# A two-layer vision tower: GpSimd's long instructions between the halves go to other engines, the routed tables come later, and the end of the routed experts is reordered

## What is computed

```python
h = patches(x) @ tokW + tokb                        # 16x16 patches, 768 -> 256
h = h + sparse_attention(layernorm(h))              # 16 heads; a router keeps 25 of 64 keys per head
h = h + moe(layernorm(h))                           # below
h = h + polymax_attention(layernorm(h))             # causal; 16 heads; score -> (1 + relu(s)**2 or 1 - 0.01 s) / 1000
h = h + ternary_ffn(layernorm(h))                   # RMS norm, w in {-1, 0, 1}, 256 -> 1024, gelu, RMS norm, -> 256

def moe(x):                                         # 8 experts in 4 groups, top 2 groups, top 2 experts
    shared = (silu(x @ sw1.T) * (x @ sw3.T)) @ sw2.T
    routed_in = x[flat_idx] * weights               # rows by the token's own index ...
    h = silu(grouped_mm(routed_in, w1, counts)) * grouped_mm(routed_in, w3, counts)
    return shared.at[flat_idx].add(grouped_mm(h, w2, counts))   # flat_idx holds expert numbers 0..7
```

## Time and profile before

| what | value |
|---|---|
| median of 3 runs | 785.64 us (785.05 to 787.7) |
| profiled execution | 786.8 us, its span 784.6 us |
| PE busy | 684.2 us (87%) |
| DVE busy | 616.3 us (79%) |
| ACT busy | 429.7 us (55%) |
| POOL busy | 114.6 us (15%) |
| mean granted clock of PE | 0.948 of full speed |

### The profile page before, as it was taken

One profiled execution on the slowest core, in us unless ns is written; L12 is line 12 of the kernel. 1 busy time (PEld: TensorE's weight loads), 2 busy tenths in 40 slices (PEclk: granted clock), 3 DMA queues, 4 the chain that ended last, 5 costly groups with the idle time before them and its releaser, 6 DMA issues.

```text
span 784.6 us, 26966 instructions
## 1 busy us (share of the span) xinstructions
PE 684.2 (87%) x11581; PEld 489.3 (62%) x11581; DVE 616.3 (79%) x1349; ACT 429.7 (55%) x661; POOL 114.6 (15%) x95
## 2 busy tenths in 40 slices
PE   5769989999999989987999698899989998798666
PEld 4455676857666675856587375575757676464534
DVE  6768888888898888889796788888889786757643
ACT  4444555464644546366473666849486662936323
POOL 0202111020212111024300421010100101010010
PEclk9889999999999999999978899999999999999959
DMA  9116202002020200020000000000000000000000
GB/s 304 55 31 239 83 0 80 0 0 80 0 80 0 80 0 0 20 91 2 1 3 2 1 7 26 3 29 1 27 0 27 0 4 28 3 29 2 29 1 28
DMA packets 8546, 27.40 MB, mean 35 GB/s; under 512 B 3616, under 2 KB 4384, under 8 KB 6944
## 3 DMA queue, kind: packets, MB, share of 16 engines
q1 hardware_dynamic: 8480, 26.42, 9.4%
HBM read 22.22 MB, written 4.19 MB: 34 GB/s over the span
## 4 chain that ended last, share of the span: by engine, by line
issue 43%; PE 30%; ACT 12%; DVE 10%; POOL 4%; DMA 1%; POOLq 0%; ACTq 0%; DVEq 0%; SPq 0%
PE PS L380 5%; PE PS L727 3%; PE PS L773 3%; ACT w_s L1076 3%; PE PS L761 3%; PE PS L717 2%; PE PS L370 2%; POOL H L1192 2%; PE PS L740 2%; ACT work L1067 2%; ACT xn L1014 1%; PE PS L391 1%; POOL rstd L1175 1%; PE PS L601 1%; PE PS L347 1%
## 5 line engine op out<-in xcount | busy, mean ns | idle before, releaser
L927 ACT ACTIVATE PT<-PS 128x512 f32<-128x512 f32 x64 | 36.6, 596 | 66.0 <-PE PS L479 66.0
L740 PE MATMUL PS<-xT,wqkv_h 128*128 128x512 f16 x256 | 65.1, 403 | 8.6 <-DVE xT L1814 4.6
L370 PE MATMUL PS<-ident_s,xn 128*128 128x128 f32 x256 | 43.3, 305 | 24.2 <-DVE xn L1348 12.3
L329 PE MATMUL PS<-tokW_h,w_s 128*128 128x256 f16 x504 | 58.5, 273 | 0.0
L920 ACT ACTIVATE Pm<-Pm 128x1024 f32<-128x1024 f32 x32 | 33.0, 1053 | 37.9 <-DVE Pm L1433 37.9
L740 PEld LDWEIGHTS PS<-xT,wqkv_h 128*128 128x128 f16 x256 | 23.6, 102 | 48.4 <-ACT w_s L1076 15.5
L445 PE MATMUL PS<-kM,qT 32*64 32x128 f32 x2048 | 52.3, 295 | 0.0
L329 PEld LDWEIGHTS PS<-tokW_h,w_s 128*128 128x128 f16 x504 | 48.6, 98 | 5.9
L370 PEld LDWEIGHTS PS<-ident_s,xn 128*128 128x128 f32 x256 | 32.0, 152 | 31.4 <-ACT vbuf L1043 13.1
L1336 DVE BATCH_NORM_STATS2 st<-H 128x6 f32 (+1 forms) x128 | 46.5, 414 | 2.6
L380 PE MATMUL PS<-xT,wat_h 128*128 128x512 f16 x192 | 44.5, 390 | 1.6 <-DVE xT L1745 1.6
(11 more groups left out here) (254 smaller groups left out, 1636.8 us busy)
## 6 DMA issues: line engine op xcount, KB each, us to landing
work<-in_x SPq DMA_DIRECT2D x7, 1536.0 KB, 6.3
out<-H SPq DMA_DIRECT2D x8, 512.0 KB, 2.6
w_s<-in_w SPq DMA_DIRECT2D x3, 1024.0 KB, 7.2
work<-in_x SPq DMA_DIRECT2D x3, 512.0 KB, 5.4
wup_s<-in_wup SPq DMA_DIRECT2D x1, 1024.0 KB, 6.2
wdn_s<-in_wdn SPq DMA_DIRECT2D x1, 1024.0 KB, 6.9
w_s<-in_tokW SPq DMA_DIRECT2D x3, 256.0 KB, 4.6
wup_s<-in_wqkv SPq DMA_DIRECT2D x1, 768.0 KB, 7.6
```

The lines of the kernel that those rows point to most:

```text
L329: m = pe.matmul(dst, halves_[xi][:, k, rows], w[:, wi, k, cols], start=(n == 0), stop=(n == 3 * chunks - 1))
L370: m = pe.transpose(PS[:, bank, t * P:(t + 1) * P], xn[:, t, c * P:(c + 1) * P], ident_s[:, :])
L740: m = pe.matmul(PS[:, UP_BANKS[f % 3], :], wup_h[:, c, f * P:(f + 1) * P], part[:, c, :], start=(k == 0), stop=(k == 2 * C - 1))
L927: act.activation(PT[:, t % 2, 4 * half:4 * half + 4, :], PS[:, TURN_BANKS[t][half], :], ACT.Copy)\
```

## The change

It has three parts.

First half: `p_bias` goes behind `p_mask` in GpSimd's loop. Behind the loop the two compares go to VectorE (`negatives`), one ahead of the split of the second norm's rows and one ahead of the second `ternary`; the zeros go to ScalarE, as one activation over the 1024 columns that are not written otherwise, ahead of `a_B1_k(0)`.

Slot 0: both tables, in banks 0 and 1, and the turn, in bank 2, are made behind the second projection, ahead of the remaining value tiles of slot 1. The transposes of slot 1 go into banks 6 and 7 and no longer wait for the scores; ScalarE copies the turned values and these rows between its two score tiles. The group choice and the choice of the best expert move behind the statistics of the first and the second pair of tiles. PE's wait for the tables moves from the projections to the scores of slot 1.

Slot 5: the sums are turned ahead of the second projection, `w2` is multiplied behind the value tiles, `gated_sums` comes ahead of the first tiles' normalization, `v_x4T` ahead of `stats3`, and ScalarE's `a_norm3` of slot 7 moves into slot 6, ahead of the copies of that slot's transposed rows.

The diff, cut to its core:

```diff
+        SECOND_BANKS = (6, 7)
...
+        def x3_banks(g):
+            if not isinstance(g, int) or g > 1:
+                return X3_BANKS
+            return SECOND_BANKS if g else FIRST_BANKS
...
@@ tensor engine
-            def routed_table(n, w):
+            def routed_tables():
                 pe.wait_ge(loaded_experts, 16 * len(loads_experts))
-                for e in range(NX):
-                    for c in range(C):
-                        at = 64 * n + e * NX
-                        m = pe.matmul(PS[:, 7, at:at + NX], w[:, e, c, :], x8[:, c, :],
-                                      start=(c == 0), stop=(c == C - 1))
-                m.then_inc(tab_mm, 1)
-
-            def table_turn():
-
+                pe.wait_ge(lin_ok, 3)
+                for n, w in enumerate((w1_s, w3_s)):
+                    for e in range(NX):
+                        for c in range(C):
+                            m = pe.matmul(PS[:, n, e * NX:(e + 1) * NX], w[:, e, c, :], x8[:, c, :],
+                                          start=(c == 0), stop=(c == C - 1))
+                    m.then_inc(tab_mm, 1)
                 pe.wait_ge(tabT_ok, 1)
-                pe.transpose(PS[0:64, 7, 128:128 + P], AC[0][:, :], ident_s[:, :]).then_inc(tab_t, 1)
+                pe.transpose(PS[0:64, 2, 0:P], AC[0][:, :], ident_s[:, :]).then_inc(tab_t, 1)
...
-            def routed_out():
+            def gate_turn():
                 pe.wait_ge(racc_ok, LAST - 2)
                 pe.matmul(PS[:, 0, 0:64], racc[:, :], fold[:, :], start=True, stop=True).then_inc(gT_mm, 1)
+
+            def routed_out():
+
                 pe.wait_ge(gT_ok, 1)
...
@@ B1_qk
-                    elif not first(g) and c == 0:
-                        pe.wait_ge(tabT_ok, 2)
-                        pe.wait_ge(tab_ok, 1)
-                        pe.wait_ge(tab_lo_ok, 1)
...
             def slot_B(g, prev, nxt, routed=None, ahead=True):
-                if not prev:
-                    routed_table(0, w1_s)
                 B2_scores(g, 2)
                 B2_scores(g, 3)
...
                 else:
-                    table_turn()
-                    routed_table(1, w3_s)
                     pe.wait_ge(h3_ok, 2 * SLOTS + 1)
                     B2_values(g, 0)
                 if nxt:
-                    pe.wait_ge(lin_ok, 3 * g + 3)
+                    if prev:
+                        pe.wait_ge(lin_ok, 3 * g + 3)
                     for c in range(C):
-                        transpose_chunk(g + 1, c, xn1, X3_BANKS[c], xn3_ok, x3T_mm)
+                        transpose_chunk(g + 1, c, xn1, x3_banks(g + 1)[c], xn3_ok, x3T_mm)
...
                     B1_v(g + 1, (0,))
+                if routed == "last":
+                    gate_turn()
                 B2_proj(g, 1, 4)
+                if not prev:
+                    routed_tables()
                 if routed in ("first", "batch"):
                     routed_gates(g)
-                elif routed:
+                if nxt:
+                    B1_v(g + 1, range(1, TILES))
+                if routed == "last":
                     routed_out()
                 if nxt:
-                    B1_v(g + 1, range(1, TILES))
                     pe.wait_ge(Bv_out, 2 * g + 3)
...
                 transpose_in(g, xn2, 6, xn4_ok, x4T_mm)
                 if nxt:
+                    if not prev:
+                        pe.wait_ge(tabT_ok, 2)
+                        pe.wait_ge(tab_lo_ok, 1)
@@ scalar engine
             def slot_B(g, prev, nxt, routed=None, ahead=True):
                 if not prev:
-                    table_out(0)
                     a_norm3(g + 1)
                 for t in (2, 3):
                     relus(g, t)
                     quads(g, t)
                     lins(g, t)
-                if not prev:
-                    table_out(1)
-                    table_turned()
-                a_turned(g, 0)
-                if nxt:
+                    if not prev and t == 2:
+                        a_turned(g, 0)
+                        a_B1_x(g + 1)
+                if prev:
+                    a_turned(g, 0)
+                if nxt and not ahead:
+                    a_norm3(g + 1)
+                if prev and nxt:
                     a_B1_x(g + 1)
...
                     a_norm3(g + 2)
+                if not prev:
+                    routed_tables()
                 if nxt:
                     a_B1_v(g + 1, 0)
                 if routed in ("first", "batch"):
                     routed_tanh(g, 0)
-                if routed == "last":
-                    a_norm3(g + 2)
                 a_B3_x(g)
...
             turns(LAST, 1)
+            act.wait_ge(pv_mm, 2 * TILES * SLOTS)
+            act.activation(V2q[:, :, 1:3, :], ones[:, 0:HD].unsqueeze(1).unsqueeze(1).broadcast_to([P, 2 * NH, 2, HD]),
+                           ACT.Copy, scale=0.0).then_inc(V2_zero, 1)
             a_B1_k(0)
             a_B1_q(0, (0,))
             x4_high(LAST)
             a_B1_q(0, (1,))
-            act.wait_ge(V2_zero, 1)
@@ gpsimd
             with pool.Fori(0, LAST) as i:
                 p_rstd1(i + 1)
-                p_bias(i + 1)
                 p_rstd(ve2_ok, i + 1, ve2, rstd2, rstd2_ok)
                 p_mask(i + 1)
+                p_bias(i + 1)
             p_rstd(ve3_ok, 1, ve, rstd, rstd3_ok)
-            pool.wait_ge(th_set, 2)
-            for n, w in enumerate((wup_f, wdn_f)):
-                pool.tensor_scalar(spare[:, n, :], w, nthr[:, n:n + 1], None, ALU.is_lt).then_inc(th_neg, 1)
             for p in range(2):
                 ts = slice(2 * p, 2 * p + 2)
                 pool.wait_ge(ve2_ok, LAST + p + 1)
                 pool.tensor_tensor(rstd2[:, ts], ve2[:, ts], mhalf[:, ts], ALU.pow).then_inc(rstd2_ok, 1)
-            pool.wait_ge(pv_mm, 2 * TILES * SLOTS)
-            pool.memset(vbuf[:, :], 0.0).then_inc(V2_zero, 1)
@@ vector engine
+            def negatives(n, w):
+                dve.tensor_scalar(spare[:, n, :], w, nthr[:, n:n + 1], None, ALU.is_lt).then_inc(th_neg, 1)
...
             def slot_B(g, prev, nxt, routed=None, ahead=True):
...
-                if not prev:
-                    table_low()
...
                     sums_in(g)
+                if routed == "last":
+                    gated_sums()
                 if not prev:
-                    best("m", "oh1", "m1", "c1")
+                    group_choice()
                 norm4(g, 0)
...
-                if routed == "last":
-                    gated_sums()
                 if routed in ("first", "batch"):
                     gates_in(g, (0,))
+                if not prev:
+                    best("m", "oh1", "m1", "c1")
                 norm4(g, 1)
+                if not prev:
+                    table_low()
                 if routed in ("first", "batch"):
                     gates_in(g, (1,))
                 elif routed:
                     routed_rows_in()
+                v_x4T(g)
                 if routed == "last":
                     stats3(g + 2)
                     minus_mean3(g + 2)
-                v_x4T(g)
...
             last_norm2(1)
+            dve.wait_ge(th_set, 2)
+            negatives(0, wup_f)
             x2_low(LAST)
...
+            negatives(1, wdn_f)
             ternary(1, wdn_f, wdn_t)
             empty_sums()
-            group_choice()
             slot_B(0, False, True)
```

More of the change, by code:

```diff
@@ L988, in _, with routed_tables @@
             slot_A(LAST - 1, False)
[L990 to L994 removed]
+            def routed_tables():
+                for n in range(2):
+                    act.wait_ge(tab_mm, n + 1)
+                    act.activation(AC[n][:, :], PS[:, n, 0:64], ACT.Copy).then_inc(tabT_ok, 1)
                 act.wait_ge(tab_t, 1)
[L996 removed]
+                act.activation(tabA[:, 0, :], PS[0:64, 2, 0:P], ACT.Copy).then_inc(tab_ok, 1)
             def count_out():
@@ L1025, in a_B1_x @@
                     act.wait_ge(x3T_mm, 2 * g + c + 1)
-                    bank = (FIRST_BANKS if first(g) else X3_BANKS)[c]
+                    bank = x3_banks(g)[c]
                     act.activation(x1_hi[:, c, 0:TOK], PS[:, bank, :], ACT.Copy).then_inc(x3T_a, 1)
@@ L1685, in table_low @@
                 dve.wait_ge(tab_ok, 1)
[L1686 removed]
+                dve.tensor_tensor(tabA[:, 1, :], PS[0:64, 2, 0:P], tabA[:, 0, :], ALU.subtract)\
                    .then_inc(tab_lo_ok, 1)
```

6 lines of the change are left out of this document (removed).

## The result

The changed kernel takes 764.75 us (median of 4 runs, 764.28 to 765.94) against 786.2 for the kernel before (4 runs): a ratio of 0.9728, 95% interval 0.9707 to 0.975. That is 21.4 us faster where 18.2 were forecast, and inside the range. The profiled execution took 764.32, with a span of 762.1; the span of before was 784.6, so the two traces differ by 22.5 us.

A forecast was written before the change was run, and what follows sets the result against it. The tensor engine (PE) was taken as the bound, losing time at four places; 8.5 + 3.0 + 2.2 + 4.5 = 18.2 us off the profiled 786.8 gave 768.6, 767.4 on the median's scale, stated as 768, range 761 to 776.

The forecast's parts named there:

- First half: Bias sum behind the mask: VectorE's add no longer held, seven PE waits 1.21 us shorter each, 8.5 us (5.5 to 10).
- 0.1 us of room: First half: bias sum ends at 312.01, VectorE's split with two SBUF inputs starts at 312.12, leaving 0.1 us.
- Between the halves: Compares and zeros leave GpSimd: the residual add shortens, PE's gap and the clock loss behind it go, 3.0 us (1.6 to 3.3).
- The cover: Between the halves: the first compare stands where VectorE idled 2.92 us; without that cover it would cost 2.35.
- Head of the second half: Tables moved behind the second projection, with VectorE reaching the split 5.0 us earlier: 2.2 us (-0.5 to 6.2).
- to come back with the dense values: Head of the second half: the clock falls again within the moved tables and recovers at the value matmuls; part taken as 2.2 us.
- Routed end: End of the routed experts: sums turned early, rows split before the norm, FFN starts 5.0 us earlier; 4.5 taken (2 to 6).
- the first: Rival: PE's waits are taken by other waits in the same slots, no change to speak of, 785 us; chance 0.04.
- the fourth: Rival: the routed end only shifts its wait into the next slot, 772.5 us; chance 0.04.
- The second: Rival, first half: the bias sum's stall only moves to the split, 1.2 us a slot, 776.5 us; chance 0.12.
- The third: Rival, head of second half: clock stays low from tables through scores, part gives -0.5, 770.7 us; chance 0.10.
- The fifth: Rival, first half: the moved bias sum holds all of VectorE for 2.35 us, PSUM readers too; slower, 796 us; chance 0.03.

The follow-up runs named there:

- The early load: Changed kernel with the third slot's patches loaded ahead of the second half's weights, not behind them: 762.75 us, ratio 0.9697 to the kernel before.
- the routed end alone: Kernel before with only the routed slot's new order (sums turned early, rows split ahead of the third norm): 780.15 us, ratio 0.9925.
- the added instruction: Changed kernel with a second GpSimd instruction of the same shape behind each bias sum of the first half: 777.39 us, ratio 0.9896 to the kernel before.

## Why the prediction was right, and where it was not

**First half, 8.5 us forecast, 9.54 measured.** The mechanism was right: the add was held by GpSimd's bias sum, and all seven waits became 1.25 us shorter (1.21 forecast). But the first of them gained nothing by it: PE then met a wait of 3.30 us for `h1T`, which stands on ScalarE behind the third slot's patches. The early load shows that this was it. ScalarE had waited for these patches in the kernel before too:

```profile
73.59 2.86 ACT L960 ACTIVATE w_s<-work 128x1536 f16<-128x1536 f32 x2 [4.00 <-DMA work<-in_x]
```

PE reached that slot's shared projections at 82.57 instead of 83.44, and these 0.87 us are the difference between 72.72 and 73.59; without the early load that copy starts between 71.48 and 74.83 in twelve traces, so they can't be told from chance. The forecast looked at one slot in the middle and multiplied by seven; the slot that shares its time with the loads was another case. What made up for it was the clock: at 248.94 the kernel before ran the same twelve matmuls in 4.23 us instead of 3.00, and the changed one has no such fall. 0.87 + 6 x 1.25 + 1.23 = 9.6. The forecast had read one slot for this as well (3.00 us behind the gap) and costed no loss. Over the traces, the twelve matmuls took over 4.2 us behind three of the 14 gaps of 1.5 us (4.45 at 70.52 and 4.23 at 248.94 in the kernel before, 4.45 in that with the routed end alone) and 3.00 or less behind all 84 gaps of 0.3. The loss goes with the gap, but how often an execution pays it is chance: that the total came so near to the forecast was partly luck.

The "0.1 us of room" for the split was 0.14, and what missing it costs is measured: 1.39 us a slot behind the added instruction. The forecast left out why the room was so small: the mask ahead of the bias sum is itself held. It starts 0.16 us behind this instruction of VectorE with two SBUF inputs and lasts 2.06 us, against 0.61 and 0.67 in the first and the last slot, where none of that length runs beside it:

```profile
307.44 1.75 DVE L1523 TENSOR_TENSOR w_s<-work,w_s 128x1536 f16<-128x1536 f32 x1
```

**Between the halves, 3.0 forecast, 3.34 measured.** 1.61 of it is the gap and 7.01 - 5.35 = 1.66 the clock behind it, the forecast's upper bound. The compares were mis-sized: each took 1.28 us on VectorE, not 2.35. The cover was right (VectorE idled 2.36 us behind the first), and so the size cost this part of the forecast nothing.

**Head of the second half, 2.2 forecast, 2.38 between the traces, 0.63 where the part alone is undone.** Here the number came out and the working did not: that was luck. VectorE reached the split 6.1 us earlier beyond the shift of the stages ahead (417.35 to 398.34, less 12.88), against 5.0 forecast; the second compare, 1.07 us shorter than taken, is the difference. But the forecast let the first tables go at no price, and their place was taken by waits: 2.12 us ahead of the scores, then 1.05 and 1.22 ahead of the values; the clock fell there, and fell again in the tables. And "to come back with the dense values" was wrong: the 18 value matmuls took 3.90 us, not 2.13 as in the kernel before. Nor are the tables PE's bound in their new place: left out, PE waits for the norm's chain through VectorE and ScalarE, and comes to the next slot no sooner. The forecast had set this chain at 3.1 us and some short instructions against 7 to 11 us of tables; it is about as long as the tables. What of the 2.38 is the edit and what the clock's chance is not settled; by the overlapping ranges of the traces it could be nothing.

**Routed end, 4.5 forecast, 7.01 between the traces: a mis-sized term, above its bound of 6.** The FFN starts 5.35 us earlier beyond the shift of 15.41 (670.62 to 649.86), against 5.0. From there to the next slot's projection it took 26.85 us before and 25.19 now, 1.66 less where 0.5 more was forecast. Some was given back: PE now waits 0.28 and 0.36 us for ScalarE and VectorE ahead of the Gram products, and the four normalizations moved into the next slot cost it 0.16. Not costed at all was the rest: the FFN's matmuls no longer run partly at half clock (8.75 us, now 3.61 + 0.42 + 4.04), and a pause of 2.29 us in the Gram products, with a fall of the clock behind it, shrank to 0.38. That pause goes with the order at this place: 2.04 to 2.32 us in the three traces with the norm first, 0.36 to 1.23 in the ten with the rows first and the tables kept. Why it is there is not settled. The forecast took the two edits as one; the turn of the sums alone pays nothing.

**What the forecast missed as a whole** is that a wait removed pays twice where the clock had fallen behind it. By the profiles' spans and mean clocks, (1 - 0.948) x 784.6 = 40.8 us of clock were withheld before and (1 - 0.959) x 762.1 = 31.2 after: up to 9.6 of the 22.5 us came from there. Over all timed executions the mean clock was 0.943 to 0.956 for the kernel before and 0.953 to 0.964 for the changed one, so the difference of one pair is no fixed price. The forecast's sum had (3.0 - 1.6) + (2.2 + 0.5) = 4.1 of it.

Of the rivals, the first and the fourth fell at once. The second's mechanism exists and misses by 0.14 us. The third is half seen: the clock stayed low from the tables through the values and was back for the scores; that this part brings nothing is not excluded. The fifth fell with the instructions that kept their 0.69 us.

## What to carry to other kernels

When a stall recurs in a loop, cost its first and last pass by themselves: the pass that runs beside the loads may hold another wait just behind the one removed. Before moving a GpSimd instruction, look which VectorE instructions with both inputs in SBUF start while it runs; a hold shows as the duration of the VectorE instruction, not as idle time, and 0.14 us of room was enough. Of two edits made together, undo each by itself: here putting one norm back took all 7 us of the stage away, so the turn of the sums alone brought none. Before reading a difference of 1 or 2 us in one stage, look how far the same stage differs between traces of kernels that share it.

## What the runs showed of the hardware that was not expected

- The compare on VectorE (one 2048-column SBUF input, one scalar per partition) takes 1.28 us; the ternary instruction of the same columns with two inputs takes 2.35.
- A VectorE instruction with two SBUF inputs waited until GpSimd's instruction was through (longest of one split 2.27 us, usual 0.69), also when GpSimd only read one 256-column row again and again; one with an operand in PSUM was not held (0.69). The other way round, GpSimd's mask took 2.06 us behind such an instruction of VectorE, 0.61 and 0.67 without.
- Leaving out some 60 of PE's instructions made the program 10 us slower, by pauses of 2 to 3 us far behind them. Four transfers of the instruction queue were the only ones in the 20 us around the first, and the stretch had 31 of them instead of 14; that PE waited for code is likely and not shown. The Trainium skill (Runtime: NRT & Kernel Launch, "Instruction fetch mechanics") calls the cost of crossing a block of instructions mostly hidden; if these pauses are such crossings, the 2.79 and 2.31 us differ from it. They lie inside a hardware loop, in two of its three passes.
